# Routing of tokens to experts moved from a stage of its own into the attention loop

## The chip, the cores and the metric

One NeuronCore of a Trainium2 chip (trn2) runs the whole program. The metric is the device time of one execution in microseconds (us). A NeuronCore has five engines that run side by side, each with its own queue of instructions: PE (TensorE, matmuls and transposes), DVE (VectorE), ACT (ScalarE), POOL (GpSimd) and SP (SyncE, which issues most DMAs here). They wait for each other by semaphores.

## The reference, cut to what matters

Shapes: x is 32 batches of 112 tokens of 512 numbers (3584 tokens), the context is 32 x 375 x 512, there are 16 heads of 32 numbers and 8 experts with a hidden width of 352.

```
x = x + attention(layernorm(x), context)      # 8-bit dynamic quantization of x and o, float32 K and V
h = layernorm(x)
logits = h @ router_w.T                       # 3584 x 8
probs = softmax(logits); vals, idx = top_k(probs, 2); vals = vals / sum(vals)
for each expert e:                            # only tokens with e in idx have a weight
    gate, up = split(h @ gate_up[e].T, 2)
    out += weight[:, e] * ((silu(gate) * up) @ down[e].T)
x = x + out
```

## The kernel before, in words

**prepare_weights** quantizes wq and wo, splits wk and wv into a high and a low part (three float32r products stand for one float32 product), and makes constants.

**attention** goes over the batches in a software pipeline. Iteration `it` computes the 16 heads of batch `it` (scores, softmax, turning of the probabilities, values), and beside them the projections of batch it+1 (K, V and Q), the end of batch it-1 (its last values, quantization of o, the product with wo) and the end of batch it-2 (residual, second layernorm, h2, router logits), and it prefetches for it+2 and it+3. It runs from it = -3 to 33; 26 iterations are a loop on the device with two bodies. The order is written out by hand: each engine has one body, a loop over h = 0 to 15, in which every piece of work has its place by h. An engine works through its own body in that order, so a step that stands ahead of another on the same engine delays it even when they have nothing to do with each other.

PE's work on K and V is 28 steps in 7 units (4 for K, 3 for V; L581 to L598), two steps or so per h, into two PSUM banks by turns. Unit u may start only when unit u-2 has left its bank: ACT writes k_hi (L409) and DVE k_lo (L490) at h = 3, 5, 7 and 9. At h = 6 PE starts unit 3, which needs k_lo of unit 1, written by DVE at h = 5; at h = 4 it starts unit 2, which needs k_lo of unit 0, written at h = 3, behind h_s (L481) of batch it-2.

Q goes through one more PSUM bank, `misc`: the product with wq at h = 7 (L637), q_tok by DVE at h = 8 (L498), the bias by POOL (L358), the turning by PE at h = 9 (L602). The logits of batch it-2 come by PE at h = 5 (L626, also in misc) and are copied by DVE at h = 5 (L485) into a table of all batches.

Batch it-2's residual is added by POOL (x_s, L345), which then helps DVE with the reciprocal root (rstd, L348 and L350), after which DVE writes h_s. POOL's last work of an iteration is w_lo (L376): attention also splits the expert weights, a 32nd part per iteration (w_raw loaded by SP, w_hi by ACT at h = 12, w_lo by POOL, four stores by SP), and puts the parts into DRAM.

**route** (L688 and on) starts when attention has ended. On all 3584 tokens at once it picks the two best experts (ties go to the lower one), makes shares by an exponential and powers, counts and ranks the tokens of each expert by two matmuls with triangular and all-one matrices, gives each expert a number of tiles of 128 slots, and finds which token sits in which slot by 64 matmuls of one-hot matrices. Its results are the tables gather and scatter (token of each slot), expert (of each tile), pair and last, and in DRAM the shares by token. SP loads the weights of experts 0 and 1 in this stage. **experts** then works through 63 tiles: POOL gathers 128 rows of h2 by an indirect DMA (L982), PE turns them, multiplies with gate_up and down in three products each, ACT and DVE make the activation, ACT scales by the share of the token (gathered by a second indirect DMA, L994), and POOL adds the rows to the output by a third (L989). Weights of expert e+2 are loaded when expert e's tiles are done.

Memory: attention's tensors are released before route and experts get theirs, so experts' weight buffers could not be filled during attention.

## Time and profile before

| | |
|---|---|
| median of 3 runs | 1616.57 us (1613.74 to 1618.61) |
| the profiled execution | 1616.73 us, span 1615.0 us |
| PE busy | 1501.2 us (93%) |
| DVE, ACT, POOL busy | 899.4, 881.5, 660.9 us |
| mean granted clock of PE | 0.970 |
| attention loop, one iteration | some 32.6 us |
| last logits to first expert tile on PE | 1120.4 to 1164.6 us |

A row of a timeline gives start and duration in us, the engine, the line of the kernel, the operation, and what it writes and reads; in brackets how long the engine was idle before it, and who released it. PEld is the loading of the stationary operand, beside PE.

### The profile page before, as it was taken

The page shows a single profiled execution, that of the slowest core. Times are in us where ns is not written, and L with a number is a line of the kernel's source. Part 1 is how long each engine was busy: PE and PEld are TensorE (multiplying, and loading weights), DVE is VectorE, ACT ScalarE, POOL GpSimd, SP SyncE. Part 2 cuts the span into 40 slices and gives each one's busy share as a digit, 9 for nine tenths or more (in the row PEclk, how much of TensorE's full clock was granted, in tenths as well). Part 3 has the DMA queues.
Part 4 walks back from the last instruction along what each step waited for, and adds up shares of the span by engine and source line. Part 5 has one row for each costly group of instructions (what it writes and reads, how often), then busy time and mean ns, then how long its engine had stood idle before and what let it go on. Part 6 is the DMA issues. An engine that isn't in the chain of part 4 may idle for free. (4 is left out here: it accounts for less than half of the span.)

```text
span 1615.0 us, 40110 instructions
## 1 busy us (share of the span) xinstructions
PE 1501.2 (93%) x11594; PEld 1310.1 (81%) x11595; DVE 899.4 (56%) x2365; ACT 881.5 (55%) x2097; POOL 660.9 (41%) x671
## 2 busy tenths in 40 slices
PE   2899999999999999999999999983399999999896
PEld 2778888888888888888888888872299999999895
DVE  6557666766676667666776667654722222222221
ACT  2467667676767676676667667761033333333232
POOL 4233334333343234333333343323555555656453
PEclk9999999999999999999999999996599999999998
DMA  5567777677767776777677767763537766666643
GB/s 175 143 168 194 209 204 193 180 224 207 188 177 222 203 194 179 212 201 205 181 199 208 207 183 189 198 168 129 171 67 186 186 155 144 150 152 127 157 78 48
DMA packets 220125, 281.09 MB, mean 174 GB/s; under 512 B 83569, under 2 KB 164977, under 8 KB 220081
## 3 DMA queue, kind: packets, MB, share of 16 engines
q1 hardware_dynamic: 203952, 247.24, 54.4%
q0 software_dynamic: 16128, 33.30, 11.8%
q8 instruction: 23, 0.38, 0.1%
q14 instruction: 22, 0.17, 0.0%
HBM read 118.31 MB, written 66.17 MB: 114 GB/s over the span
## 5 line engine op out<-in xcount | busy, mean ns | idle before, releaser
L465 DVE CUSTOM_DVE_ANT_0 probs<-score,neg_mask 112x375 f32<-112x375 f32 x512 | 279.9, 547 | 262.2 <-PE score L555 260.7
L393 ACT ACTIVATE probs<-probs,neg_max 112x375 f32<-112x375 f32 x512 | 312.2, 610 | 185.8 <-DVE neg_max L465 183.3
L386 ACT ACTIVATE probs_t<-turn 125x336 f32<-125x336 f32 x512 | 225.0, 440 | 110.1 <-PE turn L563 110.1
L563 PE MATMUL turn<-ident,probs 112*125 112x112 f32 x1536 | 265.0, 281 | 2.9 <-ACT probs L393 2.9
L563 PEld LDWEIGHTS turn<-ident,probs 112*125 112x125 f32 x1536 | 222.7, 188 | 38.0 <-issue 14.1
L555 PE MATMUL score<-k_stack,q_stack 96*112 96x376 f32 x512 | 208.4, 407 | 5.9 <-DMA q_stack<-q_lo 5.5
L590 PE MATMUL proj<-ctx_hi,wk_hi 128*128 128x376 f32 x512 | 175.6, 343 | 1.9 <-PEq L29 1.1
L590 PE MATMUL proj<-ctx_hi,wk_lo 128*128 128x376 f32 x512 | 171.9, 336 | 0.0
L590 PE MATMUL proj<-ctx_lo,wk_hi 128*128 128x376 f32 x512 | 171.9, 336 | 0.0
L1031 DVE TENSOR_TENSOR a_lo<-a_ps,a_hi 128x384 fp32r<-128x384 f32 x63 | 35.1, 558 | 244.4 <-ACT a_hi L1006 244.4
L595 PE MATMUL proj<-wv_lo,ctx_hi 128*125 128x512 f32 x384 | 151.7, 395 | 0.0
L595 PE MATMUL proj<-wv_hi,ctx_hi 128*125 128x512 f32 x384 | 151.5, 395 | 0.0
L595 PE MATMUL proj<-wv_hi,ctx_lo 128*125 128x512 f32 x384 | 151.4, 394 | 0.0
L355 POOL TENSOR_SCALAR neg_mask<-neg_mask 112x375 f32<-112x375 f32 x32 | 16.8, 525 | 292.1 <-DMA neg_mask<-mask 292.1
L371 POOL TENSOR_TENSOR ctx_lo<-ctx_stage,ctx_hi 128x1504 fp32r<-128x1504 f32 x31 | 106.5, 3436 | 58.7 <-ACT ctx_hi L430 58.7
L989 POOL DMA_INDIRECT out<-y_rows,scatter_idx x63 | 101.9, 1618 | 57.5 <-POOL scatter_idx L985 51.6
L376 POOL TENSOR_TENSOR w_lo<-w_raw,w_hi 128x1056 fp32r<-128x1056 f32 x32 | 79.0, 2469 | 71.8 <-ACT w_hi L435 71.8
L590 PEld LDWEIGHTS proj<-ctx_hi,wk_hi 128*128 128x128 f32 x512 | 97.4, 190 | 8.3 <-issue 1.5
L1019 ACT ACTIVATE y_rows<-y_ps,row_share 128x512 f32<-128x512 f32 x63 | 43.5, 691 | 106.7 <-PE y_ps L1101 83.5
L575 PE MATMUL out_t<-probs_t,v 125*32 125x112 f32 x3072 | 100.7, 264 | 0.5 <-ACT probs_t L386 0.5
L590 PEld LDWEIGHTS proj<-ctx_lo,wk_hi 128*128 128x128 f32 x512 | 97.6, 191 | 0.0
L575 PEld LDWEIGHTS out_t<-probs_t,v 125*32 125x32 f32 x3072 | 69.6, 110 | 34.3 <-issue 29.9
(198 smaller groups left out, 3419.9 us busy)
## 6 DMA issues: line engine op xcount, KB each, us to landing
k_stack<-k_hi SPq DMA_DIRECT2D x512, 94.0 KB, 2.2
k_stack<-k_lo SPq DMA_DIRECT2D x256, 94.0 KB, 2.3
ctx_stage<-ctx_t SPq DMA_DIRECT2D x32, 750.0 KB, 5.3
q_stack<-q_hi SPq DMA_DIRECT2D x256, 56.0 KB, 2.0
w_raw<-gate_up_t SPq DMA_DIRECT2D x32, 352.0 KB, 3.1
gate_up_dram_hi<-w_hi SPq DMA_DIRECT2D x32, 352.0 KB, 5.5
gate_up_dram_lo<-w_lo SPq DMA_DIRECT2D x32, 352.0 KB, 5.9
gate_up_hi<-gate_up_dram_hi SPq DMA_DIRECT2D x16, 704.0 KB, 4.9
```

Source lines behind the costliest of these rows:

```text
L371: pool.tensor_tensor(c_lo[:, par % 2, :, :], stage[:, :, :], c_hi[:, par % 2, :, :].bitcast(F32), ALU.subtract).then_inc(c_lo_made, 1)
L376: pool.tensor_tensor(w_lo[:, :], w_raw[:, :], w_hi[:, :].bitcast(F32), ALU.subtract).then_inc(w_lo_made, 1)
L386: act.activation(probs_t[:, h % RING_T, :, :], turn[h % 2][0:LC, 0:LT * N].rearrange("p (l n) -> p l n", l=LT), ACT.Copy).then_inc(turned_ ...
L393: act.activation(probs[:, h % DS, :], probs[:, h % DS, :], ACT.Exp, bias=neg_max[:, par % 2, h:h + 1], scale=-1.0, accum_out=total[:, par ...
L465: dve.tensor_tensor_reduce(probs[:, h % DS, :], score[h % 2][0:N, 0:L], neg_mask[:, p, :], 1.0, BIG, ALU.add, ALU.min, neg_max[:, p, h:h + ...
L555: pe.matmul(score[h % 2][0:N, 0:LP], q_st[:, par % 2, h, :], k_st[:, h, :], start=True, stop=True).then_inc(scored, 1)
L563: mm = pe.transpose(turn[h % 2][0:LC, l * N:(l + 1) * N], probs[:, h % DS, l * LC:(l + 1) * LC], W["ident"][0:N, 0:N])
L575: mm = pe.matmul(out_t[QUARTER * i:QUARTER * i + QUARTER, g * N:(g + 1) * N], v[:, par % 2, l, QUARTER * h:QUARTER * h + QUARTER], probs_t ...
L590: mm = pe.matmul(bank[:, 0:LP], W[w][:, t, 128 * u:128 * u + 128], c[:, q, t, :], start=(t == 0 and w == "wk_hi" and c is c_hi), stop=(t = ...
L595: mm = pe.matmul(bank[0:LC, :], c[:, q, t, l * LC:(l + 1) * LC], W[w][:, t, :], start=(t == 0 and w == "wv_hi" and c is c_hi), stop=(t == ...
L989: pool.indirect_dma_start(out, bass.IndirectOffsetOnAxis(ap=si[par][:, 0:1], axis=0), y[:, par, :], None, compute_op=ALU.add).then_inc(sca ...
L1019: act.activation(y[:, other, :], y_ps[other][:, 0:C], ACT.Copy, scale=share[:, other:other + 1]).then_inc(y_made, 1)
```

## The change

- The choice of two experts is made per batch in the attention loop. DVE gets 15 small steps and a copy with a maximum in place of the copy of logits, at h = 5, 6, 7, 8, 10 and 11, each ahead of the other work of its h (but behind the score step). PE gets two small matmuls at h = 9 for the ranks of the batch's tokens (their result lies in the free end of the bank out_t), a wait before the values at h = 10, and one count matmul at the end. POOL gets the subtraction of the two logits, four small steps and a power, and two indirect DMAs that scatter (token, share) entries of 8 bytes into a table of slots in DRAM, a region per expert; all but the subtraction stand behind w_lo. ACT gets an exponential of 112 numbers at h = 12 ahead of w_hi.
- `route` is gone. At the end of attention's own block stands the count matmul and a table of 17 DVE steps (tiles per expert, expert of tile, slots of tile).
- Expert weight buffers are allocated for the whole program; wk, wv, the context parts and k_hi, k_lo live inside them. SP loads expert 0 at the end of iteration 31 and expert 1 after the last stores of h2.
- The split of expert weights comes one iteration earlier.
- `experts` gathers entries by tile (token and share together), and then rows by the entry; the gather of shares and the two copies of indices go. Empty slots name row 3584, which is zero in h2 and lies behind the output's rows; the table of slots and these rows are filled in prepare_weights.

```
 # prepare_weights: SP
+            sp.wait_ge(no_token_made, 2)
+            for empty in slots.rearrange("(c p a) v -> c p (a v)", p=128, a=SLOTS):
+                sp.dma_start(empty, no_token[:, :, :].rearrange("p a v -> p (a v)")).then_inc(W["slots_cleared"], 16)
+            sp.wait_ge(zeroed, 1)
+            sp.dma_start(h2[T:T + PAD_ROWS, :], zero[:, :]).then_inc(W["pads_cleared"], 16)
+            sp.dma_start(pad_rows, zero[:, :]).then_inc(W["pads_cleared"], 16)
 # attention: SP
+                if not inside and it == B - 1:
+                    sp.wait_ge(unit_out, UNITS * B)
+                    sp.wait_ge(w_stored, 64 * B)
+                    load_expert(sp, R, 0)
             iterations(sp, body)
+            for half in range(2):
+                sp.wait_ge(k_stacked[half], 16 * KDMAS * B)
+            load_expert(sp, R, 1)
+            sp.wait_ge(W["pads_cleared"], 32)
 # attention: POOL
+                if has_m2:
+                    need(pool, routed, ROUTE * m2 + 5)
+                    need(pool, grown_made, m2)
+                    pool.tensor_tensor(gap[:, :], top[1][:, :], top[0][:, :], ALU.subtract).then_inc(weighing, 1)
+                if has_n:
                     need(pool, q_out, 3 * n + 2)
...
+                if has_m2:
...
+                    need(pool, entered, 32 * m2)
+                    waited(pool)
+                    pool.tensor_copy(entry[:, :, 0], W["token"][:, 0:1].to_broadcast([N, 2])).then_inc(weighing, 1)
+                    need(pool, weighing, WEIGH * m2 + 2)
+                    waited(pool)
+                    pool.tensor_scalar(W["token"][:, :], W["token"][:, :], 1.0, float(N), ALU.mult, ALU.add).then_inc(weighing, 1)
+                    need(pool, grown_made, m2 + 1)
+                    waited(pool)
+                    pool.tensor_scalar(grown1[:, :], grown[:, :], 1.0, 1.0, ALU.mult, ALU.add).then_inc(weighing, 1)
+                    need(pool, weighing, WEIGH * m2 + 4)
+                    pool.tensor_tensor(entry[:, 0, 1:2].bitcast(F32), grown1[:, :], W["minus_one"][0:N, :], ALU.pow).then_inc(weighing, 1)
+                    need(pool, weighing, WEIGH * m2 + 5)
+                    pool.tensor_tensor(entry[:, 1, 1:2].bitcast(F32), grown[:, :], entry[:, 0, 1:2].bitcast(F32), ALU.mult).then_inc(weighing, 1)
+                    need(pool, weighing, WEIGH * m2 + 6)
+                    need(pool, routed, ROUTE * m2 + 15)
+                    waited(pool)
+                    for i in range(2):
+                        pool.indirect_dma_start(slots, bass.IndirectOffsetOnAxis(ap=at_i[i][:, 0:1], axis=0), entry[:, i, :], None).then_inc(entered, 16)
             iterations(pool, body)
+            pool.wait_ge(entered, 32 * B)
 # attention: ACT
+                    if h == 12 and has_m2:
+                        need(act, weighing, WEIGH * m2 + 1)
+                        act.activation(grown[:, :], gap[:, :], ACT.Exp).then_inc(grown_made, 1)
 # attention: DVE
                     if h == 5 and has_m2:
                         need(dve, r_made, 2 * m2 + 2)
-                        dve.tensor_copy(W["logits"][0:N, bass.ds(m2, 1), :] if inside else W["logits"][0:N, m2:m2 + 1, :],
-                                        misc[0:N, 0:8].rearrange("p (a e) -> p a e", a=1)).then_inc(r_out, 1)
+                        need(dve, weighing, WEIGH * (m2 - 1) + 1)
+                        waited(dve)
+                        dve.tensor_tensor_reduce(lg[:, :], misc[0:N, 0:E], W["zeros"][0:N, :], 1.0, -BIG,
+                                                 ALU.add, ALU.max, top[0][:, :]).then_inc(r_out, 1)
+                        need(dve, r_out, 2 * m2 + 2)
+                        dve.scalar_tensor_tensor(weighed[:, :], lg[:, :], top[0][:, 0:1], W["prio"][0:N, :],
+                                                 ALU.is_equal, ALU.mult).then_inc(routed, 1)
+                        need(dve, routed, ROUTE * m2 + 1)
+                        dve.tensor_reduce(best[0][:, :], weighed[:, :], AX.X, ALU.max).then_inc(routed, 1)
...
+                    if h == 8 and has_m2:
+                        need(dve, routed, ROUTE * m2 + 7)
+                        dve.tensor_scalar(one[:, 1, :], W["prio"][0:N, :], best[1][:, 0:1], None, ALU.is_equal).then_inc(routed, 1)
+                        need(dve, routed, ROUTE * m2 + 8)
+                        need(dve, ranked, m2)
+                        dve.tensor_tensor(taken[:, :], one[:, 0, :], one[:, 1, :], ALU.add).then_inc(routed, 1)
...
                     if h in (3, 5, 7, 9) and has_n:
                         g = h // 2 - 1
                         need(dve, k_hi_made, G4 * n + g + 1)
 # attention: PE
+                    if h == 9 and has_m2:
+                        need(pe, routed, ROUTE * m2 + 9)
+                        if has_m:
+                            need(pe, out_t_out, m + 1)
+                        pe.matmul(rank[0:N, :], W["before"][0:N, 0:N], taken[:, :], start=True, stop=False)
+                        pe.matmul(rank[0:N, :], W["ones16"][0:N, 0:N], W["taken_sum"][:, :], start=False, stop=True).then_inc(ranked, 1)
...
                     if h in (6, 10, 14) and has_a:
+                        if h == 10 and has_m2:
+                            need(pe, routed, ROUTE * m2 + 10)
                         values(it, par, h // GH - 1)
 # experts: POOL
+            for t in range(NT + 2):
+                if t + 2 < NT:
+                    fetch_rows(t + 2)
+                if t >= 2:
...
+                    pool.indirect_dma_start(out, bass.IndirectOffsetOnAxis(ap=entry[:, t - 2, 0:1], axis=0), y[:, t % 2, :], None,
                                             compute_op=ALU.add).then_inc(scattered, 16)
+                if t + 4 < NT:
+                    fetch_entries(t + 4)
```

## Rows read from the trace of the kernel before

**Rows 1.** Busy time by stretch; us, then busy us (x instructions), PEclk, DMA share, GB/s

```profile
core 0: us, PE busy (x) PEld busy (x) DVE busy (x) ACT busy (x) POOL busy (x), PEclk, DMA share, GB/s
700.00:732.50 32.50, 32.50 (x281) 27.75 (x280) 22.32 (x64) 22.84 (x58) 11.67 (x11) 1.00 0.73 199
1170.00:1615.00 445.00, 425.39 (x2509) 397.07 (x2507) 119.76 (x251) 138.79 (x252) 244.51 (x307) 0.98 0.60 132
```

**Rows 2.** Timeline, from the last logits to the first expert tile

```profile
1120.36 0.17 DVE L485 COPY logits<-misc 112x8 f32<-112x8 f32 x1 [3.40 <-PE misc L626]
...
1158.90 0.20 DVE L875 CAST scatter<-number 128x64 int32<-128x64 f32 x1
1159.63 0.19 POOL L978 COPY gather_idx<-gather 128x1 int32<-128x1 int32 x1 [7.24 <-POOLq L688]
...
1160.82 1.25 POOL L982 DMA_INDIRECT rows<-h_rows,gather_idx  x1 [1.00 <-POOL gather_idx L978]
...
1164.56 1.11 PE L1092 MATMUL h_ps<-ident,rows 128*128 128x128 f32 x4 [8.08 <-DMA rows<-h_rows,gather_idx]
```

**Rows 3.** Timeline of the loop, h = 5 and 6: logits, k_lo, unit 3

```profile
725.02 0.17 DVE L485 COPY logits<-misc 112x8 f32 x1 [1.11 <-PE misc L626]
725.13 0.61 DVE L490 SCALAR_TENSOR_TENSOR k_lo<-proj,bk_col,k_hi 128x376 fp32r<-128x376 f32 x1
...
725.82 0.41 PE L590 MATMUL proj<-ctx_hi,wk_hi 128*128 128x376 f32 x1
726.07 0.33 PE L590 MATMUL proj<-ctx_lo,wk_hi 128*128 128x376 f32 x1
```

**Rows 4.** Timeline of the loop, h = 8 and 9: q_tok

```profile
730.75 0.75 DVE L498 SCALAR_TENSOR_TENSOR q_tok<-misc,x_scale,wq_row 112x512 f32<-112x512 f32 x1
...
731.58 1.29 POOL L358 TENSOR_TENSOR q_tok<-q_tok,bq_row 112x512 f32<-112x512 f32 x1 [2.08 <-DVE q_tok L498]
...
732.92 0.31 PE L602 MATMUL misc<-ident,q_tok 112*128 112x112 f32 x1
```

**Rows 5.** Timeline of the loop, from w_lo to unit 2

```profile
709.88 2.47 POOL L376 TENSOR_TENSOR w_lo<-w_raw,w_hi 128x1056 fp32r<-128x1056 f32 x1 [2.02 <-ACT w_hi L435]
716.52 1.28 POOL L345 TENSOR_TENSOR x_s<-y,x_res 112x512 f32<-112x512 f32 x1 [4.17 <-DVE y L470]
...
719.48 0.55 POOL L350 TENSOR_TENSOR rstd<-var_eps,minus_half 112x1 f32<-112x1 f32 x1
...
720.36 0.54 DVE L481 TENSOR_SCALAR h_s<-x_s,mv,rstd 112x512 f32<-112x512 f32 x1
720.82 0.60 DVE L490 SCALAR_TENSOR_TENSOR k_lo<-proj,bk_col,k_hi 128x376 fp32r<-128x376 f32 x1
...
721.56 0.36 PE L590 MATMUL proj<-ctx_hi,wk_hi 128*128 128x376 f32 x1
```

**Rows 6.** Timeline of route: small dependent steps, and the comparison for the table

```profile
1128.18 0.17 DVE L831 TENSOR_SCALAR cnt_i<-until 128x8 int32<-128x8 f32 x1
1128.39 0.17 DVE L832 TENSOR_SCALAR cnt_i<-cnt_i 128x8 int32<-128x8 int32 x1
...
1154.46 0.68 DVE L857 TENSOR_TENSOR past<-iota,last 128x512 f32<-128x512 f32 x1
```

**Rows 7.** Timeline of the loop, h = 6: four bf16 transposes

```profile
726.41 0.37 PE L602 MATMUL misc<-ident,x_int 112*128 112x112 bf16 x4
```

**Rows 8.** Groups of instructions: shapes xcount, busy us and mean ns, idle before

```profile
L989 POOL DMA_INDIRECT out<-y_rows,scatter_idx x63 | 101.9, 1618 | 57.5 <-POOL scatter_idx L985 51.6 <-ACT y_rows L1019 4.0 <-issue 1.9
L982 POOL DMA_INDIRECT rows<-h_rows,gather_idx x63 | 61.4, 975 | 57.1 <-POOL gather_idx L978 53.1 <-issue 2.2 <-DMA out<-y_rows,scatter_idx 1.9
```

**Rows 9.** Timeline of the preparation: VectorE beside a busy and an idle POOL

```profile
9.52 3.72 DVE L123 TENSOR_SCALAR w_shifted<-raw_q,w_inv 128x512 f32<-128x512 f32 x4
...
21.74 1.67 DVE L123 TENSOR_SCALAR w_shifted<-raw_o,w_inv 128x512 f32<-128x512 f32 x4
```

**Rows 10.** Timeline of iteration 32: logits and o_tok

```profile
1104.86 0.17 DVE L485 COPY logits<-misc 112x8 f32<-112x8 f32 x1 [2.99 <-PE misc L626]
...
1106.35 0.69 DVE L526 TENSOR_TENSOR o_tok<-misc,inv_total 112x512 f32<-112x512 f32 x1 [1.17 <-PE misc L602]
```

More of the change, by code:

```diff
@@ L27, in prepare_weights @@
     D = C // H
-    N = W["tokens"]
+    N, T = W["tokens"], W["rows"]
     with ExitStack() as ctx:
@@ L158, in _, with attention @@
                 mm.then_inc(row_made, 1)
-def attention(nc, W, x, ctx_t, mask, x1, h2):
+def attention(nc, W, R, x, ctx_t, mask, x1, h2, slots):
     B, N, C = x.shape
@@ L217, in attention @@
         WG, WD = W["gate_up_flat"].shape[1] // B, W["down_flat"].shape[1] // B
-        w_raw, w_hi, w_lo = sb("w_raw", [128, WG + WD]), sb("w_hi", [128, WG + WD], F32R), sb("w_lo", [128, WG + WD], F32R)
+        w_raw = sb("w_raw", [128, WG + WD])
+        w_hi, w_lo = sb("w_hi", [128, WG + WD], F32R), sb("w_lo", [128, WG + WD], F32R)
+        NT = R["tiles"]
+        NTP = NT + NT % 2
+        lg, rest, nobest = sb("logits", [N, E]), sb("rest", [N, E]), sb("nobest", [N, E])
+        weighed, slot = sb("weighed", [N, E]), sb("slot", [N, E])
+        top, best = [sb(f"top{i}", [N, 1]) for i in range(2)], [sb(f"best{i}", [N, 1]) for i in range(2)]
+        one, taken = sb("one", [N, 2, E]), sb("taken", [N, E], BF16)
+        chosen, at = sb("chosen", [N, 2, E]), sb("at", [N, 2])
+        at_i = [sb(f"at_i{i}", [N, 1], I32) for i in range(2)]
+        gap, grown, grown1 = sb("gap", [N, 1]), sb("grown", [N, 1]), sb("grown1", [N, 1])
+        entry = sb("entry", [N, 2, 2], I32)
+        cnt_i, tiles, last, jump = sb("cnt_i", [128, E], I32), sb("tiles", [128, E]), sb("last", [128, E]), sb("jump", [128, E])
+        expert, place, pair, at_t = sb("expert", [128, NTP]), sb("place", [128, NTP]), sb("pair", [128, NTP]), sb("at_tile", [128, NTP])
+        place_i = sb("place_i", [128, NTP], I32)
+        rank = out_t[:, G4 * N:G4 * N + E]
         ctx_in, x_in_ld, x_res_ld, mask_in = W["ctx_in"], W["x_in_ld"], sem("x_res_ld"), sem("mask_in")
@@ L878 @@
+            pe.wait_ge(routed, ROUTE * B)
+            pe.matmul(rank[:, :], W["ones16"][0:N, :], W["taken_sum"][:, :], start=True, stop=True).then_inc(counted, 1)
 EXPERT_DMAS = 8
@@ L901, in load_expert, with experts @@
                 issued += 1
-def experts(nc, W, R, h2, weights_by_token, out):
+def experts(nc, W, R, h2, slots, out):
     NT = R["tiles"]
@@ L921, in experts @@
         gate_ps, up_ps, y_ps = [[bank(f"{n}_ps{i}") for i in range(2)] for n in ("gate", "up", "y")]
-        rows, cw = sb("rows", [128, 2, C]), sb("cw_rows", [128, 2, E])
-        gi, si = [sb(f"gather_idx{i}", [128, 1], I32) for i in range(2)], [sb(f"scatter_idx{i}", [128, 1], I32) for i in range(2)]
+        rows, entry = sb("rows", [128, 2, C]), sb("entries", [128, NT, 2], I32)
         share = sb("row_share", [128, 2])
@@ L951, in exists @@
             return inside or 0 <= t < NT
-        def column(table, t, inside):
-            return table[:, bass.ds(t, 1)] if inside else table[:, t:t + 1]
         def expert_of(eng, t, inside):
@@ L1145, in program @@
-        for part in ("hi", "lo"):
-            R[f"gate_up_dram_{part}"], R[f"down_dram_{part}"] = gate_up_dram[part], down_dram[part]
-            R[f"gate_up_{part}"] = sb(f"gate_up_{part}", [128, 2 * (C // 128) * F2], F32R)
-            R[f"down_{part}"] = sb(f"down_{part}", [128, 2 * FT * C], F32R)
-        route(nc, W, R, weights_by_token, out[T:T + PAD_ROWS, :])
-        experts(nc, W, R, h2, weights_by_token, out)
+            W.update(stage=sb("ctx_stage", [128, 4, LP]), x_in=sb("x_in", [N, 2, C]))
@@ L1153 @@
+            prepare_weights(nc, W, x, ctx_t, wq, wk_t, wv_t, wo, bq, bk, bv, bo, router_t, slots, h2, out[T:T + PAD_ROWS, :])
+            attention(nc, W, R, x, ctx_t, mask, out[0:T, :].rearrange("(b n) c -> b n c", n=N),
+                      h2[0:T, :].rearrange("(b n) c -> b n c", n=N), slots)
+        experts(nc, W, R, h2, slots, out)
 _OUT = "out"
```

392 lines of the change are left out of this document (153 added, 239 removed).

## The prediction

> **What bounds the kernel now.** I read three views, in this order: busy time by stretch, the timeline around the seam between attention and experts, and the timeline of one iteration of the attention loop.
>
> In the stretches [rows 1] PE is busy for all 32.5 us of an iteration, at the full granted clock. An iteration lasts about 32.6 us, so whatever makes PE wait inside the loop is paid in full. In the expert part PE is busy 425 of 445 us; it bounds that too.
>
> At the seam PE has nothing to do. The last copy of router logits starts at 1120.36 and ends at 1120.53, and the first transpose of an expert tile starts at 1164.56: 44.0 us [rows 2]. Those 44 us are what the change can win.
>
> Inside the loop I looked for how close PE comes to waiting, because the change puts small VectorE steps in front of work that PE needs. Three places have no slack, and each looks alike in all 27 to 29 iterations of the steady part:
> - **Gate A, k_lo of unit 1** (h=5). Before it VectorE copies the logits. k_lo ends at 725.74, and the PE matmul that needs its bank (first step of unit 3, h=6) stands at 725.82. It takes 0.41 us where the next takes 0.33, so PE already waits 0.08 us [rows 3].
> - **Gate B, q_tok** (h=8 and 9). VectorE's q_tok starts at 730.75, directly when the score step ahead of it is through; POOL adds the bias from 731.58 to 732.87; PE turns it from 732.92, 0.05 us behind POOL's end [rows 4]; in all 32 batches that distance is 0.05 to 0.11 us, so POOL's end sets PE's start.
> - **Gate C, x_s to h_s to k_lo of unit 0** (h=0 to 4). POOL's x_s starts at 716.52, rstd ends at 720.03, h_s starts at 720.36, k_lo ends at 721.42, and PE needs it at 721.56 [rows 5]. The slack is 0.33 us between rstd and h_s, and some 0.05 us behind it.
>
> **What the change removes.** The whole route stage, between the last logits and the first gather. What is left of it in series, from the last logits on:
> - choice on VectorE, 10 small steps. Dependent small steps follow each other every 0.21 us [rows 6]: 2.1 us;
> - two rank matmuls and the way there and back: 0.8 us by estimate (two semaphore hops and 0.15 us of matmul, below);
> - 5 steps to the slot numbers: 1.1 us; the count matmul with its hops: 0.5 us;
> - the table, 17 steps: 13 small at 0.21, 4 over 64x7 or 64x8 elements at 0.7 (the same comparison takes 0.68 [rows 6]): 5.5 us. Sum 10.0 us.
> - end of the block: 0.5 us (1159.10 to 1159.63); then a gather of entries, which must land before the gather of rows starts, twice 3.7 us (1160.82 to 1164.56 [rows 2]) and 0.3 us between: 8.2 us.
>
> The last batch's two entry scatters run beside the table: choice and slots are through after about 4 us, and two issues of a microsecond and a landing end before 10 us. The sum is 18.5 us in place of 44.0: **25.5 us won**. In the tail the scatter of the last tile no longer waits for a copy of its index (1159.63 to 1160.82 shows such a copy and the gap behind it, 1.2 us; 0.3 us of issue stay): 0.9 us won.
>
> Expert 0's weights load behind the last iteration's stores, while SP has nothing else due, and expert 1's right behind the last h2 store, as before: costed at nothing, covered by the latency-bound last batches; without that cover expert 0's 8 loads would stand at the seam. The new constants and cleared slots (17 POOL steps, 5 DMAs on SP) end under VectorE's and PE's own preparation; nothing. The weight split is moved one iteration earlier: the same steps per iteration on SP, ACT and POOL, and in the prologue they meet idle engines. SP issues four stores more ahead of the second key stack of batch 0, whose scores come half an iteration later; nothing. The per-tile entry gather takes the place of the gather of shares, one DMA for one; POOL loses two copies. Nothing.
>
> **What it adds per iteration** (29 iterations, 2 to 30, have both a batch to route and one to project):
> - Gate A. A copy that also takes the maximum, a compare and a reduction replace one copy ahead of k_lo. Before: k_lo starts 0.11 us behind the copy [rows 3]. After: 0.22 + 0.21 (two dependent steps) + 0.11 = 0.54. 0.43, and 0.05 for one more semaphore step: **0.48 us**, all of it PE's wait. Bounds 0.3 (every added step at 0.11) and 0.7.
> - Gate B. Two dependent small steps before q_tok: 0.21 + 0.13 = **0.34 us**, all of it PE's. Bounds 0.22 and 0.5. POOL's new subtraction ahead of the bias is released two heads earlier and is covered.
> - Two rank matmuls of 8 columns on PE: four bf16 transposes take 0.37 us [rows 7]; two cost **0.15 us**. Bounds 0.1 and 0.25. Their wait is for a step that precedes q_tok, which PE has just waited for: nothing more.
> - Gate C. Behind w_lo (ends 712.35) POOL gets four small steps of 0.19 (as the copy in [rows 2]), a pow of 0.55 [rows 5], gaps of 0.08 (1.6 us together), a gap of 1.0 to the first indirect DMA [rows 2], and two DMAs with 0.3 between. An 8-byte scatter into DRAM is not in the trace: a gather costs 0.97 us, the scatter that adds 1.62 [rows 8]. I take 0.97, since nothing is added in flight. So 1.6 + 1.0 + 2.2 = 4.8, to 717.2, and 717.4 with the 0.2 us that the small exponential puts before w_hi on ACT. x_s is 0.9 us late, less 0.38 of slack: **0.5 us**, in 28 iterations. Bounds 0 and 1.9.
>
> The other added VectorE steps (h=6, 7, 10, 11) fall into idle time ahead of the next score: VectorE is busy 22.3 of 32.5 us [rows 1]; without that cover they would cost 0.2 us each. The 224 scatter packets per iteration use idle DMA time (share 0.73).
>
> Loop: 29 x (0.48 + 0.34 + 0.15) + 28 x 0.5 = 28.1 + 14.0 = **42.1 us lost**. Last two iterations, where nothing is projected and every step is in series: in iteration 32 choice, rank and slots (2.1 + 0.8 + 1.1) and a reciprocal of 0.25 stand between the logits and o_tok, which were 1.5 us apart (1104.86 to 1106.35 [rows 10]): 2.8 us; iteration 31 about 2 us of steps less the weight split's 1.0 us on ACT, 1.0 us. **3.8 us lost**.
>
> **A rule weighed.** When VectorE scales four 512-wide pieces while POOL subtracts, they take 3.72 us; when POOL is idle, 1.67 us [rows 9]: 0.5 us each. So the two engines hold each other up. If a DMA of entries is held up like that once per iteration, Gate C becomes 1.0 us and the sum 14 us more. The Trainium skill, "SBUF — State Buffer", section "SBUF: two separate sides", says why this speaks against the change: GpSimd cannot write the descriptors of its own DMAs while VectorE runs in a mode that takes both ports. By that rule the sum would lean to its upper side. VectorE's steps at that point read PSUM, so I leave the 14 us in the upper bound.
>
> **Sum.** The profiled execution took 1616.7 us (span 1615.0), 0.01% over the median of the runs. 1616.7 - 25.5 - 0.9 + 42.1 + 3.8 = 1636.2; I forecast **1636 us**, with 1612 to 1655 as this case's own range.
>
> **Rivals.**
> 1. *The loop swallows the steps* (the other side). If the three gates give way, the loop costs nothing: 1616.7 - 26.4 + 3.8 = 1594. It decides at 22.6 / 29 = 0.78 us per iteration; below that the kernel gets faster. For it: VectorE is idle a third of the loop. Against it: added steps stand in program order ahead of k_lo and q_tok, and PE's waits there are seen. Chance 0.15.
> 2. *POOL becomes the bound of Gate C.* Scatters of 1.62 us: 1.3 us more in 28 iterations, 36 us: 1672, and 1686 with the hold-up of 0.5 us per iteration [rows 9]. For it: the only scatter in the trace takes 1.62. Against: that one adds. Chance 0.17.
> 3. *The seam does not shrink as said* (entries, accumulating pad rows that all go to one row, or expert 0's weights are late): half the gain is lost, 1649. Chance 0.08.
>
> The forecast has 0.60. A measurement of this kernel tells 0.3%, some 5 us, from no change. Faster: rival 1 and the lowest edge of the forecast (bounds 0.3 + 0.22 + 0.1 with Gate C at zero give 18 us of loss, 1612), 0.18. Same 0.08, slower 0.74. The range of 1607 to 1670 leaves out rival 1 and the far end of rival 2.
>
> **What would show it.** Right: a wait of some 0.5 us at PE's first matmul of unit 3, 0.4 us at the turning of q_tok and 0.4 us at unit 2, an iteration of about 34.1 us in place of 32.6, VectorE's releases named as the cause, and 18 to 19 us from the last logits to the first expert transpose. Wrong: an iteration under 33.3 us (rival 1), entry scatters of over 1.5 us each (rival 2), or a seam of 30 us (rival 3).

## The result, and the profile after

The changed kernel takes 1669.2 us (median of 4 runs, 1668.0 to 1670.6); beside it the kernel before takes 1616.7 us. The ratio is 1.033, with a 95% interval of 1.031 to 1.035: slower by 52.5 us where 19.5 were forecast. The profiled execution has a span of 1666.3 us against 1615.0, 51.3 us more. It divides at four points that both traces have: the first and the last addition of q's bias on GpSimd, the last step that takes the router's logits, and the first transpose of an expert tile.

| stretch | before | after | moved | forecast |
|---|---|---|---|---|
| start to first q bias | 46.6 | 46.7 | +0.1 | 0 |
| loop, first to last q bias | 1011.0 | 1069.0 | +58.0 | +42.1 |
| end of the loop, to the last logits | 62.8 | 73.2 | +10.4 | +3.8 |
| seam, to the first expert transpose | 44.2 | 24.9 | -19.3 | -25.5 |
| experts and tail | 450.4 | 452.5 | +2.1 | -0.9 |

The loop is read first in TensorE's waits (engine, line and what it waited for: us in total, times, longest), from 130 to 1050 us. Before, this view has one row:

```profile
PE score L555 <- DMA q_stack<-q_lo: 1.6, 1, 1.6
```

After:

```profile
PE proj L766 <- DVE gate_up_lo L638: 31.7, 53, 0.8
PE misc L778 <- POOL q_tok L440: 8.4, 27, 0.3
```

k and the wide weights now lie in one buffer, so k_lo is called gate_up_lo. It is waited for twice an iteration (gates A and C), q_tok once (gate B): 40 us of waits where there were 1.6. That is two thirds of the 58.0 us by which the loop grew. The same stretch as in [rows 1], by engine (PE, PEld, DVE, ACT, POOL busy, then the granted clock, DMA share and GB/s), shows TensorE idle for 1.3 us:

```profile
700.00:732.50 32.50, 31.24 (x273) 26.49 (x274) 22.29 (x75) 20.99 (x53) 14.14 (x17) 1.00 0.67 189
```

The timeline of one iteration (start, duration, engine, line, operation; in brackets the idle time ahead and what ended it), gate A, as [rows 3]:

```profile
726.13 0.17 DVE L594 CUSTOM_DVE_ANT_0 logits<-misc,zeros 112x8 f32<-112x8 f32 x1 [1.26 <-PE misc L802]
...
726.34 0.23 DVE L597 SCALAR_TENSOR_TENSOR weighed<-logits,top,prio 112x8 f32<-112x8 f32 x1
726.60 0.16 DVE L600 TENSOR_REDUCE best<-weighed 112x1 f32<-112x8 f32 x1
726.70 0.61 DVE L638 SCALAR_TENSOR_TENSOR gate_up_lo<-proj,bk_col,gate_up_hi 128x376 fp32r<-128x376 f32 x1
...
727.36 0.44 PE L766 MATMUL proj<-down_hi,gate_up_hi 128*128 128x376 f32 x1 [0.43 <-DVE gate_up_lo L638]
```

k_lo starts 0.57 us behind the logits' step, where it was 0.11; the forecast had 0.54. Gate B, as [rows 4]:

```profile
732.31 0.23 DVE L617 TENSOR_SCALAR one<-prio,best 112x8 f32<-112x8 f32 x1
732.57 0.17 DVE L620 TENSOR_TENSOR taken<-one 112x8 bf16<-112x8 f32 x1
...
732.67 0.75 DVE L646 SCALAR_TENSOR_TENSOR q_tok<-misc,x_scale,wq_row 112x512 f32<-112x512 f32 x1
...
733.50 1.30 POOL L440 TENSOR_TENSOR q_tok<-q_tok,bq_row 112x512 f32<-112x512 f32 x1 [4.21 <-DVE q_tok L646]
...
734.86 0.31 PE L778 MATMUL misc<-ident,q_tok 112*128 112x112 f32 x1 [0.32 <-POOL q_tok L440]
```

Gate C, as [rows 5]:

```profile
710.12 2.46 POOL L458 TENSOR_TENSOR w_lo<-w_raw,w_hi 128x1056 fp32r<-128x1056 f32 x1 [2.44 <-ACT w_hi L542]
...
712.54 0.37 POOL L464 CAST entry<-token 112x2 int32<-112x2 f32 x1
...
715.47 1.04 POOL L479 DMA_INDIRECT slots<-entry,at_i  x1 [0.91 <-POOL entry L474]
...
716.81 0.94 POOL L479 DMA_INDIRECT slots<-entry,at_i  x1 [0.30 <-issue]
...
717.45 0.55 DVE L572 CUSTOM_DVE_ANT_0 probs<-score,neg_mask 112x375 f32<-112x375 f32 x1 [0.87 <-issue]
...
717.79 1.29 POOL L422 TENSOR_TENSOR x_s<-y,x_res 112x512 f32<-112x512 f32 x1
...
721.31 0.55 DVE L588 TENSOR_SCALAR h_s<-x_s,mv,rstd 112x512 f32<-112x512 f32 x1 [0.51 <-POOL rstd L427]
...
721.77 0.60 DVE L638 SCALAR_TENSOR_TENSOR gate_up_lo<-proj,bk_col,gate_up_hi 128x376 fp32r<-128x376 f32 x1
...
722.42 0.44 PE L766 MATMUL proj<-down_hi,gate_up_hi 128*128 128x376 f32 x1 [0.79 <-DVE gate_up_lo L638]
```

x_s no longer waits for y; it starts the moment GpSimd is through with the second scatter. h_s now waits for rstd (0.51 us), where before rstd was 0.33 us early.

One row here misleads. Beside the second scatter VectorE stands still for 0.87 us and the profile names no releaser ("issue"), as if the scatter held it up. It does not: the step starts 0.69 us behind the start of its score matmul on TensorE:

```profile
716.76 0.41 PE L731 MATMUL score<-k_stack,q_stack 96*112 96x376 f32 x1
```

In the kernel before, the same step had nearly the same idle time and the same distance, 0.68 us, and there TensorE is named:

```profile
716.84 0.40 PE L555 MATMUL score<-k_stack,q_stack 96*112 96x376 f32 x1
...
717.52 0.55 DVE L465 CUSTOM_DVE_ANT_0 probs<-score,neg_mask 112x375 f32<-112x375 f32 x1 [0.85 <-PE score L555]
```

The seam in the timeline, as [rows 2]:

```profile
1188.88 0.17 DVE L594 CUSTOM_DVE_ANT_0 logits<-misc,zeros 112x8 f32<-112x8 f32 x1 [3.58 <-PE misc L802]
...
1194.51 0.94 POOL L479 DMA_INDIRECT slots<-entry,at_i  x1 [0.30 <-issue]
...
1198.11 0.17 DVE L720 CAST last_tile<-last 128x8 int32<-128x8 f32 x1
...
1207.12 1.00 POOL L945 DMA_INDIRECT entries<-slots,slots_of_tile  x1 [11.66 <-POOLq L232]
...
1210.48 0.95 POOL L952 DMA_INDIRECT rows<-h_rows,entries  x1 [1.11 <-DMA entries<-slots,slots_of_tile]
...
1213.81 0.47 PE L1066 MATMUL h_ps<-ident,rows 128*128 128x128 f32 x1 [21.21 <-DMA rows<-h_rows,entries]
```

The idle time ahead of the first gather of entries ends with GpSimd's own queue at the block's end, line 232, of which that line's rows tell more (min, median, max ns, first and last start). A DRAIN is an instruction of the queue itself; GpSimd starts nothing behind it before it ends:

```profile
L232 POOLq COMPARE_BRANCH  x1: 41/41/41, 1200.4 to 1200.4; - x1
L232 POOLq DRAIN  x1: 5292/5292/5292, 1200.5 to 1200.5; - x1
```

The table ends 9.4 us behind the logits (forecast 10.0), and from the barrier (1206.3) to the first transpose it is 7.5 us (forecast 8.2). Between them lie 8.0 us where 0.5 were forecast: the scatters land at 1200.4, 2.1 us behind the table's end, and then GpSimd's queue drains for 5.3 us.

### The profile page after: what moved, and what is told of

The parts are those of the page before. It is cut to its first block and busy times, and to the rows that moved or that the text cites. A ratio compares the mean times of both kernels' runs of the same rounds, so it can differ in the third digit from the quotient of the medians.

```text
span 1666.3 us, 40892 instructions
## 1 busy us (share of the span) xinstructions
PE 1518.9 (91%) x11593; PEld 1314.4 (79%) x11594; DVE 935.0 (56%) x2867; ACT 889.1 (53%) x2128; POOL 733.5 (44%) x798
## 5 line engine op out<-in xcount | busy, mean ns | idle before, releaser
L766 PE MATMUL proj<-down_hi,gate_up_hi 128*128 128x376 f32 x512 | 179.0, 350 | 35.3 <-DVE gate_up_lo L638 34.2
L968 POOL DMA_INDIRECT out<-y_rows,entries x63 | 102.2, 1622 | 174.5 <-ACT y_rows L994 128.3
L766 PE MATMUL proj<-down_lo,gate_up_hi 128*128 128x376 f32 x512 | 171.6, 335 | 0.0
L766 PE MATMUL proj<-down_hi,gate_up_lo 128*128 128x376 f32 x512 | 171.6, 335 | 0.0
L771 PE MATMUL proj<-gate_up_lo,down_hi 128*125 128x512 f32 x384 | 151.9, 395 | 0.0
L771 PE MATMUL proj<-gate_up_hi,down_hi 128*125 128x512 f32 x384 | 151.8, 395 | 0.0
L771 PE MATMUL proj<-gate_up_hi,down_lo 128*125 128x512 f32 x384 | 151.7, 395 | 0.0
L766 PEld LDWEIGHTS proj<-down_hi,gate_up_hi 128*128 128x128 f32 x512 | 97.5, 190 | 54.1 <-DVE gate_up_lo L638 52.3
L453 POOL TENSOR_TENSOR down_lo<-ctx_stage,down_hi 128x1504 fp32r<-128x1504 f32 x31 | 107.2, 3458 | 63.4 <-ACT down_hi L534 63.4
L751 PEld LDWEIGHTS out_t<-probs_t,v 125*32 125x32 f32 x3072 | 70.5, 110 | 35.9 <-DVE chosen L626 10.7
L766 PEld LDWEIGHTS proj<-down_lo,gate_up_hi 128*128 128x128 f32 x512 | 97.6, 191 | 0.0
```

The source lines that it names most:

```text
L453: pool.tensor_tensor(c_lo[:, par % 2, :, :], stage[:, :, :], c_hi[:, par % 2, :, :].bitcast(F32), ALU.subtract).then_inc(c_lo_made, 1)
L751: mm = pe.matmul(out_t[QUARTER * i:QUARTER * i + QUARTER, g * N:(g + 1) * N], v[:, par % 2, l, QUARTER * h:QUARTER * h + QUARTER], probs_t ...
L766: mm = pe.matmul(bank[:, 0:LP], W[w][:, t, 128 * u:128 * u + 128], c[:, q, t, :], start=(t == 0 and w == "wk_hi" and c is c_hi), stop=(t = ...
L771: mm = pe.matmul(bank[0:LC, :], c[:, q, t, l * LC:(l + 1) * LC], W[w][:, t, :], start=(t == 0 and w == "wv_hi" and c is c_hi), stop=(t == ...
L968: pool.indirect_dma_start(out, bass.IndirectOffsetOnAxis(ap=entry[:, t - 2, 0:1], axis=0), y[:, t % 2, :], None, compute_op=ALU.add).then_ ...
```

## The experiments

The theory: the new steps cost by their place. They stand in program order ahead of three things that TensorE needs at once. The rivals: they cost wherever they stand (their number, the memory ports, the scatters' traffic), or one gate only hides the next. All times stand beside the kernel before, run on the same chip; lengths of loop, end and seam are read from the profiled run at the points of the table above.

**e1_gate_a.** VectorE, head 5; the logits' step stays ahead:

```diff
-    dve.scalar_tensor_tensor(weighed, lg, top[0], prio, is_equal, mult)
-    dve.tensor_reduce(best[0], weighed, X, max)
     dve.scalar_tensor_tensor(k_lo, proj, bk_col, k_hi, add, subtract)
+    dve.scalar_tensor_tensor(weighed, lg, top[0], prio, is_equal, mult)
+    dve.tensor_reduce(best[0], weighed, X, max)
```

> Only the compare and the reduce that follow the logits at head 5 are moved, from ahead of VectorE's k_lo to behind it; nothing is taken away. Order theory (the steps cost because TensorE's next weight-shared unit waits for what stands behind them): the wait of 0.43 us at unit 3 in each iteration goes and the period falls by about 0.6 us, 29 x 0.6 = 17 us, 1652 us. Count theory (VectorE's additional steps cost wherever they stand, through its own time or the memory ports): no change, 1669 us. Cascade theory (the same steps only meet the next gate, the clamp of x or q_tok): less than half of it comes back, 1662 us or more.

1659.4 us, ratio 1.027 [1.025, 1.028]; the loop is 11.8 us shorter (1057.2). The wait at unit 3 is gone (over the whole run 22.4 us and 29 waits for k_lo are left of 34.2 and 58). The place costs; the amount is two thirds of what was expected.

**e2_gate_b.** VectorE, head 8:

```diff
-    dve.tensor_scalar(one[:, 1], prio, best[1], is_equal)
-    dve.tensor_tensor(taken, one[:, 0], one[:, 1], add)
     dve.scalar_tensor_tensor(q_tok, misc, x_scale, wq_row, mult, mult)
+    dve.tensor_scalar(one[:, 1], prio, best[1], is_equal)
+    dve.tensor_tensor(taken, one[:, 0], one[:, 1], add)
```

> Only the two steps at head 8 (second one-hot, taken) are moved from ahead of q_tok to behind it. Order theory: TensorE's wait for the biased q_tok falls by 0.4 us an iteration, 29 x 0.4 = 11.6 us, 1657.5 us. Count theory: 1669 us. Cascade theory: the taken mask comes later and the rank's matmuls or the values after them wait instead: between 1663 and 1672 us.

1664.7 us, 1.031 [1.029, 1.033]; loop 1061.4, 7.6 us shorter. No wait for q_tok is left in the steady part, but the moved step takes seven times as long, since it now runs beside GpSimd's bias:

```profile
L647 DVE TENSOR_TENSOR taken<-one x32: 166/1228/1236, 141.1 to 1182.8; 112x8 bf16<-112x8 f32 x32
```

**e3_gate_c.** GpSimd, the entries' chain (five small steps, two scatters) from the end of the body to the next one:

```diff
     pool.tensor_tensor(rstd2, var_eps2, minus_half, ALU.pow)
+    enter(m2 - 1)
...
     pool.tensor_tensor(w_lo, w_raw, w_hi, subtract)
-    enter(m2)
```

> GpSimd's chain of a batch (token copy, token step, plus one, reciprocal, product, two scatters of entries) is moved from the end of an iteration, ahead of the residual sum, into the next iteration behind the second rstd, where GpSimd waits for the mask; the same instructions, the same DMAs. Order theory: h's normalisation and the k_lo behind it come 1.0 to 1.3 us earlier, TensorE's wait at unit 2 goes, 28 x 1.0 = 28 us, 1641 us; at the end the last batch's scatters are issued at about the same time, so the seam stays at 25 us. Count theory (the scatters cost by their descriptors, their traffic or the ports): 1665 us or more, and the wait at unit 2 stays.

1669.5 us, 1.033 [1.030, 1.035]: nothing won. The loop of the profiled run is 1072.7; that run took 1683.3 us, the longest of the four, and TensorE waits 14.0 us for expert weights in it (6.0 in the changed kernel). The wait at unit 2 went, and one of 1.1 us at unit 3 came. The logits' step starts 1.9 us (median) behind the router's first matmul, where it was 1.15. The prediction of the order theory fails here, so the new place has a price of its own.

**e4_gates_abc.** e1, e2 and e3 together.

> The three moves together. Order theory: the sum of the three, an iteration of 32.7 to 32.9 us as in the kernel before, 1669 - 29 x 2.0 = 1611 us, some 5 us under the kernel before, since the seam's gain of 19 us is kept and the end of the loop still loses 10. Count theory: above 1660 us. Cascade theory: two of the three overlap (VectorE reaches k_lo of head 5 late for either reason), so the sum falls short of the parts: 1620 to 1635 us.

1642.5 us, 1.016 [1.013, 1.018]; loop 1042.8. That is 27 us less, more than the parts give (14 us) and half of what order alone would give. The timeline at head 5:

```profile
708.42 1.04 POOL L433 DMA_INDIRECT slots<-entry,at_i  x1 [0.90 <-POOL entry L428]
...
709.68 0.86 PE L807 MATMUL misc<-router,h_t 128*112 128x8 f32 x8
709.77 0.94 POOL L433 DMA_INDIRECT slots<-entry,at_i  x1 [0.31 <-issue]
...
711.50 0.17 DVE L598 CUSTOM_DVE_ANT_0 logits<-misc,zeros 112x8 f32<-112x8 f32 x1 [1.91 <-PE misc L807]
...
711.65 0.61 DVE L631 SCALAR_TENSOR_TENSOR gate_up_lo<-proj,bk_col,gate_up_hi 128x376 fp32r<-128x376 f32 x1
...
712.32 0.43 PE L771 MATMUL proj<-down_hi,gate_up_hi 128*128 128x376 f32 x1 [0.67 <-DVE gate_up_lo L631]
```

The logits' step starts 1.82 us behind the router's first matmul; it was 1.15 us in the changed kernel and 1.01 in the one before. GpSimd issues the second scatter just then.

**e5_abc_no_scatter.** e4, and in `enter`:

```diff
-    for i in range(2):
-        pool.indirect_dma_start(slots, at_i[i], entry[:, i])
```

The waits for the scatters' landing go with them. The table of slots keeps its empty entries, so every expert tile gathers rows of zeros and the output lacks the experts' part.

> As e4 (the three moves), but the two scatters of entries of each batch are left out, and the waits for them; the steps that make the entries stay. The entries stay those of the cleared table, so every tile gathers and scatters pad rows: only the loop is read here. In e4 the period is 33.5 us where 32.7 was expected, and the first unit at head 6 waits 0.67 us for k_lo, whose step stands behind the logits' step, which starts 1.82 us after the router's matmuls where it was 1.01 us before, just while GpSimd issues the second scatter; ScalarE's copy of the turned probabilities is late by 0.3 us there too. Scatter theory (a scatter's issue holds up what the other engines wait for at that time): without it the logits' step comes 1.0 to 1.2 us after the router's matmuls, the wait of 0.67 us goes, the loop's period is 32.8 us. Step theory (the logits' step is late by the moved computation or by the wait for GpSimd's count): it still comes 1.8 us after, the period stays at 33.5 us.

1611.2 us, 0.997 [0.996, 0.999]; loop 1022.5. VectorE's waits in e4 and, below, in e5:

```profile
DVE logits L598 <- PE misc L807: 52.7, 27, 2.2
DVE probs L576 <- issue: 21.2, 16, 1.4
```

```profile
DVE logits L594 <- PE misc L802: 34.7, 28, 1.3
DVE probs L572 <- issue: 0.2, 1, 0.2
```

The scatter theory holds for the logits' step: over the steady part it starts 1.9 us (median) behind the router's first matmul in e4 and 1.15 us in e5, and the 20 us of the loop go with the scatters. The second rows show no hold-up. All 16 of these softmax steps start 0.58 to 0.63 us behind their score matmul, no later than the others, and VectorE's waits ahead of probs are 145 us in all in e4 and 150 in e5; only the named releaser differs. The seam is 17.5 us here (26.8 in e4), and the drain of GpSimd's queue is 48 ns:

```profile
L232 POOLq DRAIN  x1: 48/48/48, 1142.0 to 1142.0; - x1
```

**e6_other_places.** Nothing is left out; every step has another place.

```diff
-VectorE, head 5: logits, compare, reduce, k_lo
+VectorE, head 5: k_lo, logits, compare, reduce
-VectorE, head 7: k_lo; head 8: one[1], taken, q_tok
+VectorE, head 7: k_lo, one[1], taken; head 8: q_tok
-GpSimd: c_lo, w_lo, five small steps, two scatters
+GpSimd: c_lo, five small steps, w_lo, two scatters
```

> Other places for the same steps: at head 5 VectorE's k_lo is first and the whole choice behind it; the two steps of head 8 stand at head 7 behind k_lo (in e2 and e4, behind q_tok, the taken mask took 1.24 us beside GpSimd's q_tok, where it was 0.17 us); GpSimd's five computing steps stand between c_lo and w_lo, and its two scatters behind w_lo, where it had 3.8 us idle. Order theory: all three gates are off, period 32.7 us, 1669 - 29 x 2.1 = 1608 us. Scatter theory: as above, unless the scatters still hold up TensorE's or VectorE's waits at heads 15 to 2: then a period of 33.3 us, 1626 us. If the two scatters end after VectorE's y is ready, the residual sum is late by 0.4 us and heads 3 to 4 lose some 0.2 us of it.

1616.1 us, 1.001 [0.999, 1.002]: 53 us under the changed kernel, level with the one before. Loop 1017.5, 51.5 of the 58.0 us back; what the loop, its end and the experts still lose (6.5, 11.4 and 2.0 us), the seam wins (19.3). TensorE's waits in the steady part:

```profile
PE misc L779 <- POOL q_tok L440: 3.5, 12, 0.8
PE score L732 <- DMA q_stack<-q_lo: 1.3, 2, 0.9
```

**e7_late_wait and e8_early_expert1** take the seam apart. e7 waits for the landed entries at the start of the experts' block, e8 issues expert 1's load right behind expert 0's.

```diff
e7, GpSimd
     iterations(pool, body)
-    pool.wait_ge(entered, 32 * B)
...
+    pool.wait_ge(entered, 32 * B)
     fetch_entries(0)
e8, SP
     load_expert(sp, R, 0)
+    load_expert(sp, R, 1)
...
     iterations(sp, body)
-    load_expert(sp, R, 1)
```

> Only the wait for the landed scatters of entries is moved from the end of the attention block to the start of GpSimd's part in the experts' block; the semaphore belongs to the program. Drain theory (the 5.3 us drain at the block's end is GpSimd's own work after its indirect DMAs, and does not wait for the landing): it starts at 1195.5 instead of 1200.5 us, beside the table, ends at 1200.8, and the seam shrinks by 5 us: 1664 us. Landing theory (the drain lasts until the scatters have landed and a fixed time more): it starts earlier and lasts longer, and the barrier stays at 1206 us: 1669 us.

> Only the load of expert 1's weights is issued right behind expert 0's, in iteration 31, instead of after the iterations. Traffic theory (the last scatters of entries land at 1200.4 us, 5 us after their issue, because they are behind 11 MB of weights on the DMA engines): they land 2 to 3 us after the issue, at 1198 us, the block's end and the first gather come 2.5 us earlier: 1666.5 us. Fixed theory (landing of an indirect scatter is 5 us by itself, or the engines are as busy): no change, 1669 us.

e7: 1665.2 us, 1.031 [1.030, 1.033]; e8: 1666.0 us, 1.031 [1.030, 1.033]. These intervals touch that of the changed kernel; what tells is the seam, 22.1 and 21.6 us for 24.9. So e7 wins 2.8 of the 5 us of its first theory, and e8 comes out by its traffic theory. In e8 the last scatter lands 1.9 us behind its issue (it was 5.0), so the weights' traffic was in its way. Line 232's row for the drain in e7:

```profile
L232 POOLq DRAIN  x1: 9748/9748/9748, 1190.9 to 1190.9; - x1
```

It ends at 1200.65, 7.7 us behind the end of the last scatter's issue (1192.97); in the changed kernel wait and drain together took 10.3. In e12 it ends 5.3 us behind the issue. So it is no fixed time from the issue. In e7 and e12 no row shows when the last scatter lands, so whether the drain goes by the landing, and what it waits for, stays open.

**e9_pool_split and e10_dve_moves** are the two halves of e6, each alone.

> Only GpSimd's part of e6: its five computing steps stand between c_lo and w_lo, its two scatters behind w_lo; VectorE's steps are as in the changed kernel. Order theory: gate C alone goes, about 1.0 us an iteration, 29 us, 1640 us, where e3, with the same steps at heads 3 to 5, gave nothing. If e6's gain came from VectorE's places alone: 1665 us or more.

> Only VectorE's part of e6: k_lo first at head 5, the two steps of head 8 at head 7 behind k_lo. Order theory: gates A and B go, 0.6 and 0.4 us an iteration, 1669 - 29 x 1.0 = 1640 us, more than e1 and e2 together gave (14 us), because e1 left the logits' step ahead of k_lo and e2 put the taken mask beside GpSimd's q_tok. Count theory: 1665 us or more.

e9: 1636.7 us, 1.014 [1.012, 1.015], loop 1040.0. e10: 1639.6 us, 1.015 [1.013, 1.017], loop 1040.6. TensorE's waits of the steady part in e9 (gates A and B are left):

```profile
PE proj L767 <- DVE gate_up_lo L639: 11.6, 28, 0.4
PE misc L779 <- POOL q_tok L440: 8.3, 27, 0.3
```

and in e10 (gate C is left):

```profile
PE proj L766 <- DVE gate_up_lo L621: 21.5, 27, 0.9
```

So gate C lifted alone gives 29.0 us of the loop, and gates A and B lifted alone give 28.4 us. The two do not add up: e6, which lifts all three, gives 51.5 us and not 57.4. Whichever part is lifted second gives less, 23.1 us for gate C (e10 to e6) and 22.5 for A and B (e9 to e6). Why 5.9 us are in both was not traced.

**e11_before_scatters.** The kernel before, with e3's additions on GpSimd and nothing else.

```diff
     pool.tensor_tensor(rstd2, var_eps2, minus_half, ALU.pow)
+    pool: five small steps
+    pool: two indirect scatters of 112 entries of 8 bytes
```

> The kernel before, with GpSimd's five small steps and two scatters of 112 entries (into tables that nothing reads) added behind the second rstd, where e3 had them; VectorE's program is not touched. Scatter theory (their issue holds up what the other engines wait for at that time): the logits' copy comes 0.6 us later after the router's matmuls, k_lo of head 5 with it, and each iteration loses 0.5 to 1.0 us: 1616 + 30 x 0.7 = 1637 us. Rival (in e3 and e4 it was VectorE's own additional step and waits that came late): 1617 us, the copy still 1.0 us after the router's matmuls.

1664.3 us, 1.028 [1.024, 1.032] (four runs, 1648.5 to 1669.0): the logits' copy starts 1.75 us (median) behind the router's first matmul, where it was 1.01, so the mechanism is there; the size is more than twice the expected one. TensorE waits for k_lo 26 times (13.9 us in all) and, in 12 iterations, for q_tok, up to 2.8 us: the mask's DMA, issued beside the scatters at 713.16, is through at 720.0, some 3.4 us late, and q_tok's bias is queued behind the mask on GpSimd.

**e13_scatters_late.** The same additions at e6's places.

> The kernel before with the same five small steps and two scatters an iteration as e11 adds (1664 us, +50), but the steps between c_lo and w_lo and the scatters behind w_lo, as e6 has them. Place theory (what they cost is what waits for GpSimd's queue, for VectorE's next step or for the mask's DMA just then): period 32.7 to 32.8 us, the seam 7 us longer by the scatters' landing and GpSimd's drain if it lies on the path there, 1618 to 1626 us. Price theory (scatters cost an iteration about 1.3 us wherever they stand, by descriptors or traffic): 1655 us or more.

1631.9 us, 1.010 [1.006, 1.013]. The loop is 10.7 us longer than before, against 38.0 in e11; the seam is 7.9 us longer, in e11 8.1. That is more than the place theory's 1618 to 1626 us and far less than the price theory's 1655. The place explains 27 of 38 us; 10.7 us stay, 4.5 of them seen as scores that wait for the stacked keys, whose DMAs take 3.3 to 3.4 us to land in both runs, and 2.2 in the kernel before. It is not the scatters as such: in the changed kernel, e3, e4 and e6, with as many scatters, the stacked keys land in 2.1 to 2.2 us. The additions of e11 and e13 differ from the real ones in that they write the same 112 rows in every iteration; whether that is the reason was not tried. So these two runs bound what the scatters cost, and e5 and e14 measure it.

**e14_no_scatter.** The changed kernel without its two scatters an iteration and the waits for their landing; as in e5, the output lacks the experts' part.

> The changed kernel without its two scatters an iteration and the waits for them; all else stays. The entries stay those of the cleared table, so every tile gathers and scatters pad rows. Order theory: GpSimd's five steps (2.5 us) then fit into the 3.8 us in which it waited for y, the residual sum starts as in the kernel before, gate C goes and gates A and B stay: period 34.4 - 1.0 = 33.4 us, as with e9 (33.5 us); the seam shrinks to 17.5 us as in e5. In all 1669 - 31 - 7 = 1631 us. Rival (the small steps hold gate C as well): 1645 us.

1629.7 us, 1.010 [1.007, 1.014]; loop 1040.3, seam 17.5. Taking the scatters alone out gives what e9 gives by moving all: the five small steps fit into GpSimd's idle time, the scatters do not.

**e12_places_and_seam.** e6, e7 and e8, and the end of the loop reordered:

```diff
-iteration 32: logits, choice, rank, slots of batch 30; o_tok, o_int_t of batch 31
+iteration 32: logits of batch 30; o_tok, o_int_t of batch 31; choice, rank of batch 30
+iteration 33: slots of batch 30 behind h_s; its entries behind rstd2
```

> e6 with both seam edits (e7's later wait, e8's earlier load of expert 1), and at the loop's end the batch before last is chosen behind the clamp of o, its rank behind the last matmuls with wo, its slots behind the last h, its entries on GpSimd behind the last rstd. Order theory: the 4.5 us that these steps stood ahead of the last batch's way come back, and 3 to 4 us from the seam: 1616 - 8 = 1608 us, some 0.5% under the kernel before. Rival (the last batch's own scatter must wait for the landing of the one before, and the drain follows it anyway): 1613 us.

1608.3 us, 0.9971 [0.9957, 0.9985]: 0.3% under the kernel before, and by the two ratios 58 us under the changed kernel. The end of the loop is 67.2 us (74.2 in e6), the seam 21.3. The rival's part is real too: the last entries wait 1.7 us for the landing of the ones before.

```profile
1132.40 0.18 POOL L419 CAST entry<-token 112x2 int32<-112x2 f32 x1 [1.66 <-DMA slots<-entry,at_i]
```

## Why the prediction came out as it did

The direction, the three gates, and who releases them were right. The size was wrong: +19.5 forecast, +52.5 measured. The time lies at the very edge of the wide range (1607 to 1670) and outside the 1612 to 1655 that were this case's own, so that it lies in the wide one is luck. Of the 31.8 us by which the profiled run misses the sum, the loop has 15.9, its end 6.6, the seam 6.2 and the experts 3.0. Step by step:

- **Gate C, the term that failed most.** 0.5 us in 28 iterations, 14.0 us, was forecast; e9 and e14 both measure 29 with gate C lifted alone, and it is 23.1 with the other gates already gone (e10 to e6). The form was right (x_s's lateness less 0.38 us of slack), the lateness was mis-sized. From w_lo's end to x_s it takes 5.2 us, not 4.8: the small steps come every 0.3 to 0.6 us on GpSimd where 0.27 was taken. x_s starts 2.42 us behind the start of y (715.37), where it was 1.06 (715.46): 1.36 us late, not 0.9. 1.36 less 0.38 is the 1.0 us that the iteration loses. The scatters cost 1.0 us each to issue, as taken from [rows 8], so rival 2's reason (1.6 us) is false. Its 1672 us are nearer to the 1669.2 than the forecast, by luck.
- **Gates A and B.** 0.48 and 0.34 us, 23.8 us together; lifted alone they give 28.4 (e10), lifted behind gate C 22.5. About right. The waits read in the profile (0.43 and 0.32) are as forecast, and the matmul behind a wait also runs longer (0.44 for 0.33 us).
- **Rank.** 0.15 us in 29 iterations, 4.4 us; with all gates lifted, e6 leaves 6.5 us, in which q_tok is still waited for 12 times, 3.5 us in all. About right.
- **The last two iterations.** 3.8 us forecast, 10.4 measured; the reordering in e12 takes 7.0 us back. The 10.4 lie in three parts: 1.9 us to the logits of iteration 31, 4.9 from there to those of iteration 32, and 3.6 to the last ones. I counted 1.0 us for iteration 31 and 2.8 for iteration 32, where the last part alone has 3.6. In e11, which has no choice at all, the stretch is 5.4 us longer, all of it in the second part; in e14, which has the choice and no scatters, that part is 5.3 us longer too. Both have the small steps on GpSimd; what makes the second part longer was not separated.
- **The seam.** Choice, rank, slots and table: 10.0 us forecast, 9.4 measured. Gathers: 8.2 and 7.5. The block's end, 0.5 us, is the step that failed here: it takes 8.0. I let the scatters land beside the table, before 10 us; they land 11.5 us behind the logits' step. And I put the drain behind them at nothing. The trace of before had a sign of it. The drain at the end of its route stage (5.7 us) only lasts as long as the work under it, and that of its attention is 0.7 us, but neither block issues an indirect DMA on GpSimd. The experts' block does, and at its end the queue drains for 4.3 us with nothing beside it:

```profile
L916 POOLq DRAIN  x1: 4278/4278/4278, 1610.5 to 1610.5; - x1
```

  e5 and e14 show 17.5 us without scatters, my 18.5 less 1.0; from the barrier to the first transpose it takes 7.7 us in e5, so the gathers are not what is quicker.
- **Experts and tail.** -0.9 forecast, +2.1 measured. The first tile takes 14.5 us from its first transpose to its first down product, where it was 13.6, and the granted clock in the first 25.5 us is 0.83 for 0.87; TensorE had been idle for 21.2 us ahead of it, where it was 8.1. The one wait for expert weights is 6.0 us for 5.3, and the drain at the program's end 4.9 for 4.3. The copy that the last scatter no longer waits for gives 0.5 of the 0.9 us, since the scatter now waits for the landing of the one before. No run was spent on these, and their causes stay open.
- **The rule weighed.** I feared 14 us if a scatter is held up by VectorE. The 15 us came, but not so: the scatters' own times are 1.04 and 0.94 us (median of 64: 1.03). What e3, e4 and e11 show, at another place than this one, is the reverse: the logits' step on VectorE comes 0.7 to 0.8 us late (medians) beside a scatter.
- **Rival 1** (the loop swallows the steps) was false for these places and true for others: e6 is the same work in the same loop at 6.5 us. What I took for a property of the steps was one of their places.

## What to carry to other kernels

Where one engine is busy all the time, look up for each added step what stands behind it in its queue and which of the busy engine's waits that feeds; a few tenths of a microsecond there are paid in every iteration, and a place one head earlier or later, behind the gated step, can cost next to nothing (6.5 us here, where the first places cost 58.0). An indirect DMA is more than its issue: it can hold up another engine's next step and the landing of a transfer issued beside it, and it leaves a drain at the block's end, so it belongs where nobody waits. When a move wins nothing, look whether the work has only met another gate, before blaming the work. And where the profile names no releaser for a pause, compare the same step in a kernel without the suspect, by its distance from the step that feeds it, before calling the pause a hold-up.

## What the runs showed of the hardware

- **Two engines at one port.** A sum over 112x8 values takes 0.17 us on VectorE, and 1.23 us (median of 32) where it starts during GpSimd's addition of the bias; in e4 it starts at 718.18 and ends at 719.42, GpSimd's addition runs from 718.09 to 719.40. The Trainium skill, "SBUF — State Buffer", section "SBUF: two separate sides", says that a VectorE operation with two SBUF inputs and a GpSimd operation that reads SBUF lock each other out for a whole instruction. The trace agrees: the step ends when GpSimd's does. By that rule e2's place was a bad one and head 7, with GpSimd idle, a good one (e10's taken: 0.168 us).
- **A scatter can slow what is beside it.** With two scatters of 112 entries at heads 3 to 5, VectorE's logits' step starts 1.9 us (median) behind the router's first matmul in e4 and 1.15 us in e5, the same kernel without scatters; on the kernel before it is 1.75 us with scatters (e11) and 1.01 without. The mask's DMA takes 4.9 us to land in e4, and 3.5 in e5 and e6 (medians). By what path is open.
- **The drain.** GpSimd's queue drains for 5292 ns at the end of the attention block when its scatters have landed (the changed kernel, e6 and e8 alike; 5294 in e11 and e13), and for 48 ns when the block had none (e5, e14). At the end of the experts' block it is 4871 ns in the changed kernel and 4278 in the one before. On the kernel before, scatters in the loop make the seam 8 us longer (e11, e13).
